# A memset and a wait on it between the gathers of each chunk of a graph network kernel

## The reference, cut to what matters

```python
# layer 0
msg_in = concatenate([x[src], x[tgt], edge_features])
messages = relu(msg_in @ W1 + b1) @ W2 + b2
agg = segment_sum(messages, tgt) / max(counts, 1)
# layers 1, 2, 3
e = leaky_relu(a_src[src] + a_dst[dst]);  m = segment_max(e, dst)
p = exp(e - m[dst]);                      z = segment_sum(p, dst)
out = segment_sum((p / z[dst]) * h[src], dst)
# after each layer
x = layernorm(x + layer(x))
```

## Time and profile before

| | |
|---|---|
| median of 3 timed runs | 8751.18 us (8750.0 to 8758.39) |
| profiled execution, first to last instruction (span) | 12335.1 us |
| PE busy in it | 7368.8 us, 60% |
| DVE busy | 5183.6 us, 42% |
| ACT busy | 2180.5 us, 18% |
| POOL busy | 6252.3 us, 51% |
| 6448 gathers on POOL, busy | 6112.1 us, mean 948 ns |
| mean granted TensorE clock | 0.727 |

### The profile page before, as it was taken

One profiled execution on the slowest core, in us unless ns is written; L12 is line 12 of the kernel. 1 busy time (PEld: TensorE's weight loads), 2 busy tenths in 40 slices (PEclk: granted clock), 3 DMA queues, 4 the chain that ended last, 5 costly groups with the idle time before them and its releaser, 6 DMA issues.

```text
span 12335.1 us, 141293 instructions
## 1 busy us (share of the span) xinstructions
PE 7368.8 (60%) x41611; PEld 6500.9 (53%) x41612; DVE 5183.6 (42%) x13628; ACT 2180.5 (18%) x7255; POOL 6252.3 (51%) x6594
## 2 busy tenths in 40 slices
PE   5666666666565555665565555555555555565554
PEld 5655555555555545554455555554544555555554
DVE  3222222224444444444464444444445444444445
ACT  2111111112111111111121111111112111111112
POOL 4555555554455545554445555555544555555553
PEclk7777777777777777777767777777776777777776
DMA  3222222222211111111122121121112221111111
GB/s 88 55 55 55 55 54 55 56 55 59 51 47 47 47 45 47 47 46 45 46 67 48 47 48 48 48 48 48 47 47 55 49 48 48 48 48 48 48 48 42
DMA packets 425594, 625.69 MB, mean 51 GB/s; under 512 B 189754, under 2 KB 305737, under 8 KB 425285
## 3 DMA queue, kind: packets, MB, share of 16 engines
q0 software_dynamic: 206336, 462.61, 15.4%
q1 hardware_dynamic: 218910, 160.84, 5.0%
q10 hardware_dynamic: 296, 1.65, 0.0%
HBM read 598.03 MB, written 26.58 MB: 51 GB/s over the span
## 4 chain that ended last, share of the span: by engine, by line
another core or an unknown queue 29%; PE 25%; DVE 23%; issue 16%; DVEq 4%; ACT 2%; POOL 1%; DMA 0%; SPq 0%; ACTq 0%; POOLq 0%
PE ps L713 12%; PE ps L760 7%; DVE acc L1263 5%; DVE memb L1183 4%; DVEq L1237 2%; PE ps L703 2%; DVE msg L1356 2%; DVE msg L1276 1%; DVEq L1263 1%; PE ps L791 1%; DVE acc L1253 1%; DVE shared L1310 1%; PE ps L795 1%; DVE shared L1348 1%
## 5 line engine op out<-in xcount | busy, mean ns | idle before, releaser
L568 POOL DMA_INDIRECT G<-rows,idx x6448 | 6112.1, 948 | 5686.5 <-DVE msg L1356 2881.2
L713 PE MATMUL ps<-msg,memb 128*128 128x136 f32 (+2 forms) x12896 | 2052.4, 328 | 62.9 <-DVE msg L1356 62.2
L760 PE MATMUL ps<-membT,shared 128*104 128x128 f32 x9672 | 2082.8, 400 | 2.2 <-ACT membT L925 2.2
L713 PEld LDWEIGHTS ps<-msg,memb 128*128 128x128 f32 x12896 | 1976.0, 236 | 84.0 <-issue 41.1
L760 PEld LDWEIGHTS ps<-membT,shared 128*104 128x104 f32 x9672 | 1874.9, 270 | 29.5 <-issue 3.0
L703 PE MATMUL ps<-ident,memb 128*128 128x128 f32 x6448 | 1108.2, 302 | 1137.5 <-issue 750.3
L1183 DVE TENSOR_TENSOR memb<-rel,ps 128x768 f32<-128x768 f32 x1488 | 1044.4, 729 | 1509.1 <-PE ps L713 1227.7
L703 PEld LDWEIGHTS ps<-ident,memb 128*128 128x128 f32 x6448 | 770.4, 150 | 1393.4 <-issue 1034.4
L925 ACT ACTIVATE membT<-ps 128x512 f32<-128x512 f32 x1984 | 991.3, 510 | 1961.8 <-remote 1639.2
L732 PE MATMUL ps<-shared,membT 128*128 x3224 | 813.8, 336 | 754.2 <-DVE msg L1276 472.5
L1263 DVE TENSOR_TENSOR acc<-acc,ps 128x136 f32 (+2 forms) x3472 | 1023.0, 295 | 561.7 <-issue 315.5
(11 more groups left out here) (182 smaller groups left out, 4864.9 us busy)
## 6 DMA issues: line engine op xcount, KB each, us to landing
G<-rows,idx POOLq DMA_INDIRECT x6448
shared<-marks_all SPq DMA_DIRECT2D x372, 156.0 KB
shared<-in_edge_attr SPq DMA_DIRECT2D x124, 256.0 KB
shared<-in_edge_attr SPq DMA_DIRECT2D x124, 160.0 KB
rows<-msg SPq DMA_DIRECT2D x36, 288.0 KB, 2.7
idx<-in_src SPq DMA_DIRECT2D x496, 6.5 KB
xrows<-msg SPq DMA_DIRECT2D x24, 256.0 KB, 2.2
memb<-xrows SPq DMA_DIRECT2D x24, 256.0 KB, 2.9
```

The lines of the kernel that those rows point to most:

```text
L568: nc.gpsimd.indirect_dma_start(G[:, b, t, 0:rows[l].shape[1]], None, rows[l], bass.IndirectOffsetOnAxis(idx[:, b, t:t + 1], 0)).then_inc(g ...
L713: last = mm(ps_sum[k // 2][:, 0:width], memb[:, b, k * P:(k + 1) * P], msg[:, b, k, 0:width], start=k % 2 == 0, stop=k % 2 == 1 or k == K - 1)
L760: last = mm(ps_sc[b][0:JH, :], adz[:, k // 2, K - 1 - k:K - 1 - k + JH], membT[:, k, :], start=k == 0, stop=False)
```

## The change

After each gather of a chunk but the last, POOL clears a strip of 256 elements on one partition, `spacer`, which nothing reads. It counts that up on a new semaphore `spaced`, waits for it, increments `gather_paced`, and issues the next gather. The waits are for each single memset (the value rises by 12 for each chunk; inside the loops it is worked out in a register). The semaphores that count gathers are shared by layers 0 and 1 and by layers 2 and 3, with the values that are waited for raised accordingly, since the number of semaphores is limited.

```diff
+        spacer = sb("spacer", [1, 256])
...
+        spaced = sem("gather_spaced")
...
-        gathered = [[sem(f"gathered_l{l}_{b}") for b in range(2)] for l in range(4)]
+        gathered = [[sem(f"rows_gathered{m}_{b}") for b in range(2)] for m in range(2)]
...
                 pool.sem_inc(gather_paced, 1)
                 for t in range(K):
+                    if t:
+                        nc.gpsimd.memset(spacer[:, :], 0.0).then_inc(spaced, 1)
+                        pool.wait_ge(spaced, (K - 1) * (CH * l + c) + t)
+                        pool.sem_inc(gather_paced, 1)
                     nc.gpsimd.indirect_dma_start(
                         G[:, b, t, 0:rows[l].shape[1]], None, rows[l],
-                        bass.IndirectOffsetOnAxis(idx[:, b, t:t + 1], 0)).then_inc(gathered[l][b], 16)
+                        bass.IndirectOffsetOnAxis(idx[:, b, t:t + 1], 0)).then_inc(gathered[l // 2][b], 16)
...
-                act.wait_ge(gathered[l][b], 16 * K * (h + 1))
+                act.wait_ge(gathered[l // 2][b], 16 * K * (PAIRS * (l % 2) + h + 1))
```

More of the change, by code:

```diff
@@ L435, in edges @@
                     return
-                sp.wait_ge(gathered[l][b], 16 * K * (h + 1))
+                sp.wait_ge(gathered[l // 2][b], 16 * K * (PAIRS * (l % 2) + h + 1))
                 load_indices(l, c + 2, b)
```

## The result

The changed kernel takes 13,521.6 us (median of 4 runs, 13,518.6 to 13,521.7) against 8754.1 us: 1.544 times as long, 95% interval 1.542 to 1.547. The forecast was 13,300, its own range 12,400 to 14,100. The profiled execution's span is 13,519.8 us, so this time the traced and the timed execution are alike.

What follows compares the result with a forecast made beforehand. POOL's issue of gathers was taken as the bound: 592 us around the gathers plus 496 chunks of 25.6 us (12 x 2.03 + 1.25) gave 13,290, forecast as 13,300 us. Its own range was 12,400 to 14,100, the wider one 10,600 to 14,800.

Steps and rivals of the forecast that it cites:

- The bound: POOL's issue of 13 gathers, 1.249 us apart, takes 16.24 us per chunk and bounds the timed run.
- The step: From one gather's start to the next inside a chunk: 2.03 us in place of 1.249, 12 times per chunk.
- the restart: On POOL, from the end of the awaited memset to the next gather's start: 0.78 us.
- rival A: Gather restarts cheaply behind the wait, 0.18 us: chunk 18.4 us, time 9,720 us; chance 0.21 including the values between.
- rival B: Gather's 0.30 us gap is a tail added before the memset: 2.33 us between starts, 15,080 us; chance 0.12.
- The overlap that goes: On POOL, preparing the next gather while one runs, which leaves a 0.30 us gap, is lost behind a wait.
- The sum: Whole kernel: 592 us around the gathers plus 496 chunks of 25.6 us, 13,290 us.
- The slack: POOL's spare time per chunk in the timed run: 0.2 us, from 16.45 against 16.24 us.
- The remainder of 104 us: Measured time before the change above POOL's occupancy of 8647 us; if it stayed, the forecast would be 13,400 us.
- The pauses: Chain's 29% of "another core or an unknown queue", 3577 us, taken as a feature of the profiled execution only.
- Rival C: POOL's idle time ahead of each chunk takes in the added waits: time stays 8751 us; chance 0.05.
- Rival D: Spacing shortens the gathers or the chain behind them: faster, at most 104 us to be won; chance 0.02.

Runs made afterwards that it cites:

- the one-step run: Changed kernel with one memset and wait per chunk, ahead of its seventh gather, instead of twelve: 9067.1 us against 8764.2, ratio 1.035.
- six steps: Changed kernel with memset and wait ahead of every second gather, six per chunk: 11,048.9 us, 0.863 of the kernel before on the fourth chip.
- the run with the late wait: Changed kernel, but each wait is for the memset before the last, with two strips in turn: 9706.9 us, ratio 1.109 to the kernel before.

## Why the prediction was right

**The bound.** Right in three layers of four. That POOL's 16.24 us per chunk bound the timed run, argued without a trace of such a run, is what the run of the wait without a memset shows directly (16.3 us in layers 2 and 3, 16.4 in layer 0), though the trace before hid it behind 7.8 us of waiting per chunk. In layer 1 something else binds, at 17.0 us.

**The step.** 2.03 us forecast, 2.04 measured: the memset 0.305 against 0.301 us, the restart 0.78 against 0.79. The choice between 0.18 and 0.78 us for the restart decided the forecast, and the row of a gather behind a wait was the right one; the row of an ordinary instruction (rival A, 9720 us) was not, nor was the tail of rival B: waiting for the gather itself gives 1.73 us, not 2.03. The overlap that goes is named rightly too: with nearly the same instructions and a wait that is met early, 3815 us of the cost are gone. What POOL does in the 0.79 us, the prediction's "prepared", no row shows. That the register instruction is hidden holds where the wait is met at once, by the 8758.0 us; behind the memset it is hidden or inside the 0.79.

**The memset's length.** The Trainium skill ("Perfetto Trace Analysis", section "GPSIMD Engine Instruction"), by its rule to time POOL by the spacing of starts, would have made the memset 0.25 us and the sum 12,900. Here the recorded length was the better one: the steps agree with 0.301 us within 0.01.

**The sum.** 13,290 us against 13,519.8 of the profiled execution, 230 short. The largest part is what no row of before could show, the gaps of 2.11 us: POOL's waits under "issue" are 413 us in 619 cases, of which 492 starts between chunks at 0.30 us make 148. The remaining 127 take 265 us: 122 of 2.11 us, which are 161 us more than 122 restarts, and five shorter ones. The memset and the restart as measured make 0.01 us per step, 60 us, and small differences some 40 us more. Against them stands a term that was too large. The stretches around the gathers, read as in the earlier trace rows, take 558 us in the changed kernel and not 592, so 34 us of error are hidden in the good agreement. By the starts a chunk takes 26.13 us, and 558 + 496 x 26.13 gives the measured time.

**The slack.** 0.2 us per chunk was right as a mean (the one-step run took in 89 us, 0.18 per chunk) and wrong as a picture: it is 0.8 us in layer 1, where POOL does not bind, and next to nothing elsewhere. The remainder of 104 us in the working was mostly this layer.

**The pauses.** Wrong. The prediction took them for a feature of the profiled execution, because 12,335 less 29% is 8758. That agreement was luck. The chain with pauses runs through PE (25%) and DVE (23%), with POOL at 1%, while the chain of the 8756.2 us trace has POOL at 25% and "issue" at 37% (shown above with that run), so what is left without the pauses is not the same work. Timed runs have the pauses as well, on two of four chips, and in the kernels with six and twelve steps they are absent. The forecast did not suffer, as POOL's 26 us per chunk exceed either period; but the 52% that it gave over the median hold only for the chips without pauses, and on the fourth chip the change costs 5.6%. A change of less weight would have been judged by the wrong baseline on those chips, as six steps show: their 11,049 us are 14% under the 12,813 us beside them, and would be 26% over 8758 us. (They were not run on a chip without pauses.)

**Not slower, faster.** Rival C would have needed gathers 0.54 us apart; they are 1.25 in the fast run too. Rival D saw nothing to win. For this change that holds on the fourth chip too, but six steps are faster there, and a gain of that kind it did not foresee.

## What to carry to other kernels

Where gathers follow each other at a short gap, a wait for the engine's own last work costs the full restart of the next one: look for a row where the same kind of instruction starts behind a wait, and take its distance, 0.79 us for an indirect gather, not the gap between two of them in a row, 0.30. Waiting for one piece of work earlier keeps the order and nearly all of the overlap. When a span and the timed median differ by 41%, do not choose a story for it: run the kernel again, on another chip if possible, before a small change is judged against either.

## What had not been expected of the hardware

- The same program takes 8758 or 8764 us on two chips and 12,307 or 12,813 us on two others, each within 1% while it was used. The second kind shows waits for "another core or an unknown queue" (29% of the chain), 7.13 us in the row above, at hand-overs from PE; they were seen here only in kernels whose gathers follow each other without a wait.
- With a wait on POOL's own work ahead of each gather, POOL pauses 2.11 us instead of 0.79 once in 4 chunks: in the changed kernel every 104 us, in the run that waits for the gather itself every 90, in that with a memset of one element every 94. The pause stands nearly always ahead of the fifth gather of every fourth chunk, whether a memset lies between the gathers or not. At the same place the run with the late wait has 0.70 us in place of 0.16 and the run with six steps 0.82 in place of 0.30; the kernel before and the run of the wait without a memset have their usual 0.30. So it seems that POOL's running ahead hides it in part or whole. Its cause was not tried.
- The memset of 256 columns is 25 ns longer on 128 partitions than on one, while two memsets of 456 columns differ by 1 ns.
